# The local mask enters the score banks as eight small products instead of two large ones

## The reference, cut to what matters

```python
mask = (it < jb) | (it > jb + w) | (jb == -1)
sim = jnp.einsum('bhwie,bhwje->bhwij', bq, bk2) * QK_SCALE
sim = jnp.where(mask, -jnp.finfo(sim.dtype).max, sim)
attn = jax.nn.softmax(sim, -1)
out = jnp.einsum('bhwij,bhwje->bhwie', attn, bv2)
```

## Time and profile before

| what | value |
|---|---|
| time before, median of 3 runs | 4747.47 us (4742.75 to 4749.88) |
| the profiled execution, its own time | 4748.92 us |
| its span, first to last instruction | 4747.2 us |
| PE busy over the span | 4319.4 us (91%) |
| DVE, ACT, POOL busy | 66%, 57%, 55% |
| mean granted clock of PE | 0.963 of full speed |
| transformer stage, from its first mask product to its last | 262 to 3489 us |

### The profile page before, as it was taken

One profiled execution on the slowest core, in us unless ns is written; L12 is line 12 of the kernel. 1 busy time (PEld: TensorE's weight loads), 2 busy tenths in 40 slices (PEclk: granted clock), 3 DMA queues, 4 the chain that ended last, 5 costly groups with the idle time before them and its releaser, 6 DMA issues. The chain is left out here.

```text
span 4747.2 us, 156031 instructions
## 1 busy us (share of the span) xinstructions
PE 4319.4 (91%) x69192; PEld 2792.5 (59%) x69192; DVE 3144.3 (66%) x4110; ACT 2720.9 (57%) x3930; POOL 2628.5 (55%) x1468
## 2 busy tenths in 40 slices
PE   7489999999999999999999999999975999788868
PEld 5256666666666666666666666666652554344435
DVE  4477776777667776777767777777733443699974
ACT  4246666666666666666656666666642443577743
POOL 0266666666666666666666666666622112477752
PEclk8699999999999999999999999999986999899999
DMA  2111212221222112211122122211111000211110
GB/s 56 52 34 42 48 45 64 49 48 45 54 54 52 44 46 59 56 44 45 44 62 50 44 49 58 55 44 47 46 30 33 1 1 1 93 72 72 72 35 16
DMA packets 230431, 221.12 MB, mean 47 GB/s; under 512 B 137657, under 2 KB 185794, under 8 KB 227714
## 3 DMA queue, kind: packets, MB, share of 16 engines
q1 hardware_dynamic: 229761, 211.13, 17.0%
HBM read 68.50 MB, written 4.03 MB: 15 GB/s over the span
## 5 line engine op out<-in xcount | busy, mean ns | idle before, releaser
L1018 POOL TENSOR_TENSOR tf_qk<-tf_qk,tf_rot 128x1024 f32<-128x1024 f32 x384 | 909.7, 2369 | 1135.0 <-DVE tf_rot L1396 1134.3
L1084 PE MATMUL tf_psum<-tf_Wqkv,tf_xsT 128*128 128x512 f32 x1536 | 738.3, 603 | 45.3 <-issue 20.0
L1025 POOL TENSOR_TENSOR tf_qk<-tf_qk,tf_rn 128x1024 f32<-128x1024 f32 x384 | 722.6, 1903 | 63.4 <-ACT tf_rn L1277 63.4
L1270 ACT ACTIVATE tf_sq<-tf_psum 128x1024 f32<-128x1024 f32 x384 | 393.9, 1026 | 507.9 <-DVE tf_rot L1396 507.9
L1392 DVE TENSOR_TENSOR tf_qk<-tf_psum,tf_table 128x1024 f32<-128x1024 f32 x384 | 467.6, 1218 | 239.3 <-PE tf_psum L1084 235.7
L1402 DVE TENSOR_REDUCE tf_ss<-tf_sq 128x16 f32<-128x1024 f32 x384 | 457.8, 1192 | 23.4 <-ACT tf_sq L1270 23.4
L1396 DVE TENSOR_TENSOR tf_rot<-tf_psum,tf_table 128x1024 f32<-128x1024 f32 x384 | 466.4, 1215 | 0.0
L1084 PEld LDWEIGHTS tf_psum<-tf_Wqkv,tf_xsT 128*128 128x128 f32 x1536 | 271.4, 192 | 325.2 <-issue 299.3
L1066 PE MATMUL tf_psum<-ident,tf_qk 128*128 128x128 f32 x3072 | 405.5, 275 | 22.1 <-ACT tf_qT L1292 2.4
L1150 PE MATMUL tf_psum<-tf_probT,tf_Vback 64*64 64x32 f32 x12288 | 396.1, 222 | 26.6 <-DVE tf_z L1437 16.0
L1066 PEld LDWEIGHTS tf_psum<-ident,tf_qk 128*128 128x128 f32 x3072 | 344.0, 141 | 112.8 <-issue 110.6
(11 more groups left out here) (319 smaller groups left out, 7961.8 us busy)
## 6 DMA issues: line engine op xcount, KB each, us to landing
tf_Vback<-tf_V SPq DMA_DIRECT2D x384, 128.0 KB
tf_Vback<-tf_V SPq DMA_DIRECT2D x576, 64.0 KB
mb_Csb<-mb_kept SPq DMA_DIRECT2D x16, 2048.0 KB, 7.1
tf_zr<-z SPq DMA_DIRECT2D x96, 128.0 KB, 2.7
z<-tf_z SPq DMA_DIRECT2D x48, 256.0 KB, 2.5
tf_Wqkv<-in_Wqkv_split SPq DMA_DIRECT2D x18, 512.0 KB, 3.8
tf_zu<-z SPq DMA_DIRECT2D x97, 64.0 KB
tf_zu<-z SPq DMA_DIRECT2D x97, 63.5 KB
```

The costliest lines, as they stand in the source:

```text
L1018: nc.gpsimd.tensor_tensor(v, v, rot[:, kind, :], ALU.add).then_inc(added.sem, 1)
L1025: nc.gpsimd.tensor_tensor(v, v, rn[:, t, HEADS * kind:HEADS * (kind + 1)].unsqueeze(2) .to_broadcast([P, HEADS, HD]), ALU.mult).then_inc(n ...
L1084: last = nc.tensor.matmul(proj[:, half, :], xsT[:, step.unit(0), WIN + t * P:WIN + (t + 1) * P], Wqkv[:, c:c + 512], start=True, stop=True)
L1270: nc.scalar.activation(sq[:, kind, :], flat2(proj), ACT.Square).then_inc(squared.sem, 1)
```

## The change

The two products of 128 rows and 128 columns become eight of 64 rows and 32 columns, one for each window w and each bank `odd`, in the same places of the array as the score products that follow: rows 64 odd to 64 odd + 63, columns of window w. The stationary operand is a block of the bf16 identity of 64 x 32. Since bank 0 is filled from rows 0 to 63 and bank 1 from rows 64 to 127, the mask rows of each window have to lie in either half of the partitions, so there is a second copy of the mask with its halves exchanged: two more DMAs from DRAM, and a conversion to bf16 that is twice as wide. Columns, data type and repetition of the moving operand stay.

```diff
-        mask32 = sb("mask32", [P, TT, HD])
-        mask = sb("mask", [P, TT, HD], BF16)
+        mask32 = sb("mask32", [P, 2, TT, HD])
+        mask = sb("mask", [P, 2, TT, HD], BF16)
...
-            sp.dma_start(mask32[:, :, :], d["local_mask"]).then_inc(consts, 16)
+            sp.dma_start(mask32[:, 0, :, :], d["local_mask"]).then_inc(consts, 16)
+            for half in range(2):
+                sp.dma_start(mask32[64 * half:64 * half + 64, 1, :, :], d["local_mask"][64 - 64 * half:P - 64 * half, :, :])\
+                    .then_inc(consts, 16)
...
-                for odd in range(2):
-                    nc.tensor.matmul(score[:, odd, :], identb[:, :], mask[:, t:t + 1, :].to_broadcast([P, PAIRS, HD]),
-                                     start=True, stop=False, skip_group_check=True)
+                for w in range(WPT):
+                    for odd in range(2):
+                        r, c = slice(64 * odd, 64 * odd + 64), 64 * odd + w % 2 * WIN
+                        nc.tensor.matmul(score[w * WIN:(w + 1) * WIN, odd, :], identb[r, c:c + WIN],
+                                         mask[r, (w // 2 + odd) % 2, t:t + 1, :].to_broadcast([64, PAIRS, HD]),
+                                         start=True, stop=False, skip_group_check=True)
...
-            dve.wait_ge(consts, 32)
-            nc.vector.tensor_copy(mask[:, :, :], mask32[:, :, :]).then_inc(masks_ready, 1)
+            dve.wait_ge(consts, 64)
+            nc.vector.tensor_copy(mask[:, :, :, :], mask32[:, :, :, :]).then_inc(masks_ready, 1)
```

## The result

The changed kernel takes 4730.21 us in the median of 9 runs (4726.99 to 4748.58), the kernel before 4746.06 (9 runs, 4735.74 to 4756.3). The medians lie 15.9 us apart; the ratio over all runs is 0.9973, 95% interval 0.996 to 0.9985, which is 12.9 us faster, between 7 and 19. The forecast was 28.6 us. The profiled execution took 4729.12 us, 19.8 less than that of before; six of the nine runs lie between 4727 and 4733, three between 4741 and 4749, these three with a mean granted clock of 0.960 or 0.961 where the six have 0.963 or 0.964.

A forecast was written before the change was run, and what follows sets the result against it. PE was taken to bound the transformer stage; 146 steps saving 0.215 us give 31.4, less 0.9 (start), 1.1 (layer changes) and 0.8 (instruction supply): 28.6 us saved, forecast 4719 us, range 4704 to 4738.

The forecast's parts named there:

- what bounds the stage: Transformer stage: PE bounds it, busy 3136 of 3227 us, so work taken from PE shortens it except at certain waits.
- the array's own saving: Mask products in each step: eight run at once, costing one product's time, saving 0.215 us (0.14 to 0.24).
- the change of form: Switch from large to small products: 0.09 us once per step, now ahead of the mask instead of behind, no gain.
- the row halves stand in line: Rival, mask products: bf16 row halves don't overlap, two groups of four run in turn, 4749 us; chance 0.14.
- all eight: Rival, mask products: all eight stand in line, 231 us slower, 4979 us; chance 0.06 for the slower case.
- the steps with ff 3: 46 steps where `attend` waits for DVE's `add_output`: nothing gained, wait grows from 15 to about 25 us.
- the start: Head of the stage: two more DMAs in SP's queue delay the first projection by 0.9 us (0 to 1.3).
- the changes of layer: Five changes of layer: the wait for weights takes a mask's gain, at most 1.1 us in all.
- The supply of instructions: PE's instruction packets: nine more add one "issue" wait, 0.8 us; shifted packet ends could change this by +-6 us.
- the 8 us that I had set as the limit: Sign for PE's "issue" waits: a difference above 8 us would mean the supply of instructions was read wrongly.
- the lower end: Smallest-gain end of the time range: 20 us saved, with 6 of supply and 3 of the rest, gives 4738.
- The rivals: Row halves in line, 4749 us (0.14); ff 3 steps gaining too, 4708 (0.06); all eight in line, 4979 (0.06).

The follow-up runs named there:

- e1_columns: Changed kernel with its eight mask products made 128 rows by 32 columns, one bank after the other, same instruction count: 4758.57 us, 1.003 of the kernel before.
- e6: Changed kernel padded to 2816 instructions per four steps, 16 satisfied waits at stage start, packet ends fixed at bad place 150: 4800.12 us.
- e10: Same padding and bad packet ends as e6, but mask products of 128 rows by 32 columns, banks in line: 4818.61 us.
- e5: Same padded kernel as e6 except 348 satisfied waits at stage start, packet ends fixed at good place 240: 4698.01 us.
- e9: Same padding and good packet ends as e5, but mask products of 128 rows by 32 columns, banks in line: 4737.2 us.
- e7: e5 with DVE's first sum of squares moved behind second rope and output addition in steps with ff 3: 4676.44 us.

## Why the prediction was wrong

**Right: what bounds the stage, and the array's own saving.** The eight products run side by side, 0.23 us from mask to scores with the first load; the change of form costs 0.09 us once. 0.52 became 0.32: 0.205 us against a forecast of 0.215. That the row halves stand in line, or all eight, is excluded by the rows. The Trainium skill ("TensorEngine Tiling (Array Packing)", Restrictions) has column tiling turn off the fast weight load; whatever that costs, the eight loads take 0.11 us together and not the 0.21 estimated for them in line.

**Right, and shown: the steps with ff 3.** Their wait grew from 15.0 to 23.7 us (forecast 25). They kept 0.08 us, not 0; with the wait gone, 0.23. Of the 9.0 us that the array gave in these steps the wait took 8.7; the 0.08 come from elsewhere, 2.6 us less in the attend products and 2.2 less in `narrow`, with 1.2 more in the scores.

**Right in size: the start.** Forecast 0.9, measured 1.2. The 1.1 us for the changes of layer don't show: those waits for weights fell from 13.3 to 11.0 us.

**Wrong: "The supply of instructions ... 9 more packets add one, 0.8 us", with +-6 us for the places, and that the score products behind the mask stay as long as they were.** This is the step that failed. I had seen that the breaks are late instructions and priced them by number: so many per packet. They have to be priced by what they do to a gain. In the profiled execution all of PE's waits named "issue" in the stage rose from 39.0 us (14.1 in the score products, 18.7 in the attend products and 6.2 in three smaller groups) to 50.2: +11.2, outside the 8 us that I had set as the limit. e1_columns shows that neither the added instructions nor, but for the breaks with ff 0, the moved places did this, but the shorter way to the score products; e6 and e10 show how: the late packet starts with the mask, whatever the mask takes, and PE is there earlier for nothing. At the good places (e5 against e9) still a quarter of the gain is lost (0.24 of 0.32 us arrive in the mean of ff 0 to 2), with ff 1 and 2 because the 128 products with 128 loads run a little slower behind the shorter mask. That they do is shown, why is not.

The account of the profiled execution, from the starts of PE's products: in the 139 steps with ff 0 to 2 the array gave 28.7 us (41.5 in the mask, less 12.8 for the change of form ahead of it), and 14.7 arrived. The score products took 7.7 us more, 6.6 of them with ff 2, where broken steps went from 3 to 8 and the unbroken ones from 1.52 to 1.63 us in the median. The other 6.3 lie behind them: 3.3 in `output`, whose waits named "issue" rose from 0.6 to 2.9, 2.1 in the attend products with ff 0, 1.7 in `turn_probs`, and 0.7 less in `turn_part`. With 4.0 from ff 3 this is the stage's 18.7. The first mask product comes 0.9 us earlier in spite of the 1.2 us, and 0.3 are gained behind the last one: 19.9. By all runs it is 12.9, with 7 to 19 as its interval; a single pair of executions lies just outside it.

**The range.** 4730 us lies inside 4704 to 4738, and that is partly luck: the lower end had room for an array that saves only 0.14 us and for 6 us of unlucky places. The array saved its 0.205, and late packets and slower score products took 14. The lower end was also added wrongly: 4747.5 - 20.4 + 6 + 3 is 4736.

**The rivals.** Of those named, none happened. The missing rival was a second limit of the work behind the mask, close under the array's. For the breaks it is the arrival of a packet, which is shown; for the slower pace of the unbroken score products with ff 1 and 2 such a limit is only supposed.

**Open.** What starts a packet's fetch was not tried. In the steps with ff 1 of e6 and e10 it coincides with the start of the first mask product, but the packet end before also stands only ten instructions and 0.53 us ahead of that product, so either can be the start. What paces the unbroken score products was not measured by itself either. The places of e5 fit this program's count alone. That e6 and e10 differ with ff 0 by 0.38 us, more than the mask's 0.32, was not explained.

## What to carry to other kernels

A gain ahead of a burst of short instructions is only worth what the burst can take up: look in the trace at how often the burst breaks at "issue", and count a step with such a break as giving nothing, as for any other wait. Where breaks of about 1 us recur in unrolled code, count the instructions between them; if it is a multiple of 256, a few instructions more or less ahead of the loop can be worth more than a change to the work: here 102 us between two values of one constant. And a wait that appears in one kind of step only, like that with ff 3, is worth its order on the other engine before anything on the waiting one: 21 us for moving one call on the changed kernel, 13 on the kernel before.

## What the runs showed of the hardware

- PE's instructions come in packets of 256 (2304 more, nine packets more). One that is late stops PE for 0.4 to 1.9 us in e6, 1.0 in the median, and PE goes on 1.1 to 1.6 us after its transfer has ended (548 breaks in all traces). In e6 and e10 the restart lies at 2.40, 2.67, 2.94 or 3.22 us from the first mask product and hardly anywhere else: steps of 0.27 us.
- Two waits on semaphores share one instruction (the 348 waits of e5 made 174 of them); at the start of the stage one such instruction stands 0.105 us from the next at the least.
- Eight bf16 products of 512 columns in eight places take 0.23 us to the next product, those of 128 rows and 32 columns 0.54 us for two times four with a change of form behind them. 348 satisfied waits at the start of the stage put the first projection 1.1 to 1.4 us later (e7 and e5 against the changed kernel); the rest is hidden behind the loads.
